# A mixture-of-experts layer on one core: three shared groups ahead of the routed slots instead of four, five row buffers, and part of the routing moved from GpSimd to VectorE

## The chip, the core and the metric

The kernel runs on one core of a Trainium2 chip. The metric is the device time of one execution in microseconds (us). Before the change the median of three runs is 888.17 us (885.1 to 893.15). PE is TensorE (its matmuls), PEld its weight loads, DVE is VectorE, ACT is ScalarE, POOL is GpSimd, SP is SyncE, which here only issues transfers.

## What is computed

`x` has 4096 tokens of 256 values (two sequences of 2048). Three steps follow each other:

```
x = x + 0.5 * ffn(layernorm(x))          # layer 0 of the code
x = x + attn(layernorm(x))               # "attention": projection, 4-tap convolution, linear recursion, silu, projection
x = x + 0.5 * ffn(layernorm(x))          # layer 1, same weights as layer 0

ffn(x):  shared = silu(x @ wg.T) * (x @ wu.T) @ wd.T          # every token
         logits = x @ gate_w.T ; e = argmax ; score = sigmoid(max)
         routed = the same form with the weights of expert e, on x * score   # 8 experts, one per token
         return shared + routed
```

## The kernel before

**Groups.** The tokens are 32 tiles of 128, in 8 groups of 4 tiles (`NG = 8`, `GT = 4`). Every product is made of three matmuls (`mm3`, lines 383 to 385: high by high, low by high, high by low part of float32 values), so PE has most of the work. The shared part of a feed-forward layer takes one group at a time: gate and up products in four blocks `fb`, then the down product, then DVE adds it to `acc` (`add_shared`). `ORDER[L]` sets the order of the groups in layer L. The first group of each order is computed while the layer norms of the others are still being made; `half_groups(L, 0)` are then computed ahead of the routed slots, and `half_groups(L, 1)` behind them.

**Routed slots.** Tokens are sorted by expert in DRAM. A place in `xs_sorted` is worked out for each token: DVE makes the one-hot table, PE the prefix sums, DVE the sums over tiles (`slot_tables`), POOL the place itself (`token_rows`, table `pos`). SP loads a group's normalized rows from `xn_kept` into one of two buffers of `rows` (`load_rows`), DVE multiplies them by the score (`scale_rows`, at the places that `SCALED` names), POOL scatters them by four indirect transfers per group (`scatter`). When the last scatter has landed, SP loads the first slots and PE starts on the 39 slots of 128 rows (`routed_slots`). The results go to `ys_sorted`.

**The weights of an expert** come twice, as raw values (`wr_raw`) and rounded ones (`wr_hi`); the low part `wr_lo` is their difference. For expert 0 POOL makes it in three parts between scatters (`cut_part`, line 1757), for the others whole (`cut_expert`, line 1765).

**Gathers.** Behind the slots POOL gathers each tile's routed rows and adds them into `acc` (line 1792), 32 tiles per layer. In layer 1 the three groups that are computed last go into a buffer of their own (`yr`, line 1901), and DVE adds them (`add_rows`). In layer 0, 24 tiles are gathered before the loop of the attention, and 8 in its first rounds (`gather(3)` whole in round 0, the tiles of group 7 in rounds 1 to 4). Each engine runs its own instructions in the order written; they wait for each other by semaphores alone.

## Time and profile before

| | |
|---|---|
| median of 3 runs | 888.17 us (885.1 to 893.15) |
| profiled execution | 891.24 us, its span 889.4 us |
| PE busy | 843.3 us, 95% of the span |
| DVE, ACT, POOL busy | 480.9, 382.1, 460.8 us |
| mean granted TensorE clock | 0.986 |

The span runs from the first to the last instruction of the core. A row of the timeline has its start, the time that it took, engine, line, output and inputs, and in brackets the idle time before it with what ended that time. A group of the lines view has the summed time and the mean of one in ns, then the idle time before the instructions. A granted clock of 1.00 is 2.4 GHz, 0.50 is 1.2 GHz.

### The profile page before, as it was taken

Reading aid. Unit: us, or ns where it says so; the run is one execution under the profiler, and the core shown is the slowest. Engines: PE = TensorE matmul, PEld = TensorE weight load, DVE = VectorE, ACT = ScalarE, POOL = GpSimd, SP = SyncE. Lnnn points to the kernel's source line nnn. Section 1 sums busy time; section 2 is a strip of 40 time slices with the busy share of each in tenths; the row PEclk is TensorE's granted clock in tenths of the full one; section 3 lists DMA queues with packets and bytes.
Section 4 is the critical chain, followed back from the end, with each engine's and each line's share of the span. In section 5 each row is a group of like instructions: output and inputs, shape, how many; then the busy total and the mean of one; then the engine's idle time right before and its main releaser. Section 6 shows DMA issues by size and latency. Waiting matters only on the chain.

```text
span 889.4 us, 16359 instructions
## 1 busy us (share of the span) xinstructions
PE 843.3 (95%) x5398; PEld 734.9 (83%) x5399; DVE 480.9 (54%) x1012; ACT 382.1 (43%) x749; POOL 460.8 (52%) x427
## 2 busy tenths in 40 slices
PE   3999989999999999998998999999999999999993
PEld 2788878888888888887887988988888888888883
DVE  6987553333333335668998885856333333333452
ACT  3353223333333333456776776333243443434230
POOL 5627670333333008869999983477331233330685
PEclk9999999999999999997999999999999999999997
DMA  9795663445555316222011016457445555521566
GB/s 309 259 327 172 204 221 109 159 163 197 189 199 191 101 50 114 40 42 30 17 45 31 24 45 223 123 189 244 167 132 189 200 189 201 177 70 35 107 150 153
DMA packets 72695, 128.66 MB, mean 145 GB/s; under 512 B 6746, under 2 KB 64228, under 8 KB 68292
## 3 DMA queue, kind: packets, MB, share of 16 engines
q0 software_dynamic: 17536, 74.33, 26.9%
q1 hardware_dynamic: 54610, 53.63, 19.1%
q8 instruction: 32, 0.52, 0.3%
q14 instruction: 19, 0.16, 0.1%
q10 hardware_dynamic: 498, 0.02, 0.0%
HBM read 91.64 MB, written 36.32 MB: 144 GB/s over the span
## 4 chain that ended last, share of the span: by engine, by line
PE 61%; POOL 15%; DVE 8%; DMA 7%; issue 5%; ACT 2%; ACTq 0%; POOLq 0%; SPq 0%; DVEq 0%
PE bank L383 18%; PE bank L384 17%; PE bank L385 17%; POOL acc L1792 5%; PE bank L591 4%; POOL xs_sorted L1725 3%; DMA rows<-xn_kept 2%; DVE v L1429 2%; DMA xs_sorted<-rows,pos 2%; DMA wr_hi<-w_routed 2%; PE bank L560 2%; POOL v L1697 2%; PE bank L450 2%; POOL wr_lo L1765 1%; POOL yr L1901 1%
## 5 line engine op out<-in xcount | busy, mean ns | idle before, releaser
L1765 POOL TENSOR_TENSOR wr_lo<-wr_raw,wr_hi 128x3072 fp32r<-128x3072 f32 x14 | 95.3, 6807 | 95.9 <-DMA wr_hi<-w_routed 92.1
L383 PE MATMUL bank<-wr_hi,xT_hi 128*128 x312 | 130.2, 417 | 1.6 <-POOL wr_lo L1765 1.5
L384 PE MATMUL bank<-wr_hi,xT_lo 128*128 x312 | 123.8, 397 | 0.0
L385 PE MATMUL bank<-wr_lo,xT_hi 128*128 x312 | 122.9, 394 | 0.0
L1134 DVE TENSOR_TENSOR hT_lo<-bank,hT_hi 128x512 fp32r<-128x512 f32 x78 | 53.9, 692 | 124.8 <-ACT hT_hi L843 124.8
L1387 DVE TENSOR_TENSOR hf<-sg,bank 128x512 f32<-128x512 f32 x78 | 53.7, 689 | 125.1 <-PE bank L385 125.1
L1792 POOL DMA_INDIRECT acc<-ys_sorted,pos x52 | 86.6, 1664 | 54.2 <-DMA ys_sorted<-rows 39.8
L383 PE MATMUL bank<-xT_hi,ws_hi 128*128 128x512 f32 x256 | 102.2, 399 | 0.4 <-DVE ws_lo L1551 0.4
L384 PE MATMUL bank<-xT_hi,ws_lo 128*128 128x512 f32 x256 | 100.6, 393 | 0.0
L385 PE MATMUL bank<-xT_lo,ws_hi 128*128 128x512 f32 x256 | 100.5, 393 | 0.0
L843 ACT ACTIVATE xT_hi<-bank 128x256 fp32r<-128x256 f32 (+1 forms) x126 | 56.0, 464 | 99.8 <-PE bank L560 88.8
L859 ACT ACTIVATE sg<-bank 128x512 f32<-128x512 f32 x64 | 38.3, 598 | 133.3 <-PE bank L385 122.3
L383 PE MATMUL bank<-wr_hi,hT_hi 128*128 x312 | 93.8, 301 | 1.3 <-DVE hT_lo L1134 1.3
L385 PE MATMUL bank<-wr_lo,hT_hi 128*128 x312 | 87.4, 280 | 0.0
L384 PE MATMUL bank<-wr_hi,hT_lo 128*128 x312 | 87.3, 280 | 0.0
L1725 POOL DMA_INDIRECT xs_sorted<-rows,pos x64 | 65.2, 1018 | 32.7 <-issue 16.8
L1429 DVE SCALAR_TENSOR_TENSOR v<-bank,vec,v 128x511 f32<-128x511 f32 (+2 forms) x96 | 71.0, 746 | 13.7 <-ACT v L992 11.1
L922 ACT ACTIVATE sg<-bank 128x512 f32<-128x512 f32 x78 | 46.6, 598 | 69.7 <-PE bank L385 69.7
L1236 DVE TENSOR_TENSOR hf<-sg,bank 128x512 f32<-128x512 f32 x64 | 43.7, 683 | 59.5 <-PE bank L385 45.5
L383 PE MATMUL bank<-ws_hi,hT_hi 128*128 128x256 f32 x256 | 74.5, 291 | 1.4 <-DVE hT_lo L1134 1.3
L384 PE MATMUL bank<-ws_hi,hT_lo 128*128 128x256 f32 x256 | 72.9, 285 | 0.0
L385 PE MATMUL bank<-ws_lo,hT_hi 128*128 128x256 f32 x256 | 72.9, 285 | 0.0
(234 smaller groups left out, 2115.1 us busy)
## 6 DMA issues: line engine op xcount, KB each, us to landing
wr_raw<-w_routed POOLq DMA_DIRECT2D x16, 1536.0 KB
wr_hi<-w_routed POOLq DMA_DIRECT2D x16, 1536.0 KB
rows<-xs_sorted SPq DMA_DIRECT2D x78, 128.0 KB, 2.6
ys_sorted<-rows SPq DMA_DIRECT2D x78, 128.0 KB, 1.7
xn_kept<-xg SPq DMA_DIRECT2D x16, 512.0 KB, 3.6
rows<-xn_kept SPq DMA_DIRECT2D x16, 512.0 KB
xg<-xn_kept SPq DMA_DIRECT2D x12, 512.0 KB
acc<-x SPq DMA_DIRECT2D x8, 512.0 KB, 9.9
```

The costliest lines, as they stand in the source:

```text
L383: pe.matmul(o, a_hi, b_hi, start=start, stop=False, skip_group_check=True)
L384: pe.matmul(o, a_lo, b_hi, start=False, stop=False, skip_group_check=True)
L385: return pe.matmul(o, a_hi, b_lo, start=False, stop=stop, skip_group_check=True)
L843: return act.activation(o, i, ACT.Copy)
L922: act.activation(sg[:, 0, :], MG[:, :], ACT.Silu).then_inc(s_msg, 1)
L1134: return dve.tensor_tensor(o, full, f32(h), ALU.subtract)
L1236: dve.tensor_tensor(hf[:, fb % 2, :], sg[:, fb % 2, :], U2[fb % 2][:, :], ALU.mult).then_inc(s_h, 1)
L1387: dve.tensor_tensor(hf[:, 0, :], sg[:, 0, :], MU[:, :], ALU.mult).then_inc(s_mh, 1)
L1429: dve.scalar_tensor_tensor(vb_[:, d:GN], UB[cb % 2][:, 0:GN - d], vec[:, cb, k:k + 1], vb_[:, d:GN], ALU.mult, ALU.add).then_inc(s_tap if ...
L1725: pool.indirect_dma_start(out=xs_dram, out_offset=bass.IndirectOffsetOnAxis(ap=pos[:, tt:tt + 1], axis=0), in_=rows[:, half * GT + t, :], ...
L1765: pool.tensor_tensor(wr_lo[:, e % 2, :], wr_raw[:, :], f32(wr_hi[:, e % 2, :]), ALU.subtract).then_inc(s_wl, 1)
L1792: pool.indirect_dma_start(out=acc[:, tt, :], out_offset=None, in_=ys_dram, in_offset=bass.IndirectOffsetOnAxis(ap=pos[:, tt:tt + 1], axis= ...
```

## The change

- `half_groups`: three groups of each layer are computed ahead of the slots and four behind (before: four and three). The orders stay.
- Five row buffers take the place of two: the two of `rows`, and three in `more_rows`, which lies where the low part of the second expert's weights comes later. SP loads the rows of groups 2 to 4 without waiting for a scatter; groups 5 to 7 wait for the scatter of the group five before.
- POOL makes only two steps of the places (`token_ranks`), and starts them from the sums over tiles. DVE makes the rest, four instructions at the end of `slot_tables`, and a new semaphore releases the scatters.
- The three parts of expert 0's low part are made by DVE in `shared_group` (`CUT`), not by POOL. The rounded weights of expert 1 are loaded after group 5's scatters, its raw ones after the last.
- DVE scales rows at other places (`SCALED`).
- In layer 0, 28 tiles are gathered before the loop of the attention, and one tile of group 3 in each of the rounds 0 to 3. In layer 1, two groups go through `yr` instead of three.

```diff
+    ROW_RING = 5
...
-        def half_groups(L, half): return ORDER[L][1:NH + 1] if half == 0 else ORDER[L][NH + 1:]
+        def half_groups(L, half): return ORDER[L][1:NH] if half == 0 else ORDER[L][NH:]
+
+        def row_buffer(g):
+            b = g % ROW_RING
+            return rows[:, b * GT:(b + 1) * GT, :] if b < 2 else more_rows[:, (b - 2) * GT:(b - 1) * GT, :]
+
+        def row_uses(L, g): return L * len(range(g % ROW_RING, NG, ROW_RING)) + g // ROW_RING
...
 
-        LATE = half_groups(1, 1)
-        ADDED = [{}, {3: (LATE[0],)}, {2: (LATE[1],), FB: (LATE[2],)}]
-
-        GATHERED = (6, 7, LATE[0], 0, LATE[1], 1, LATE[2], 2)
+        LATE = half_groups(1, 1)[2:]
+        ADDED = [{}, {}, {}, {1: (LATE[0],), FB: (LATE[1],)}]
...
-                dve.tensor_scalar(ne[:, 2, :], before, float(P), None, ALU.mult).then_inc(s_cum, 1)
+                chained(dve.tensor_scalar(ne[:, 2, :], before, float(P), None, ALU.mult))
                 dve.tensor_copy(after_e[:, :], src[0:1, :])
+                t3 = pfx[:, 0, :, :]
+                dve.wait_ge(s_rank, L + 1)
+                chained(dve.tensor_tensor(t3, t3, ne[:, 2:3, :].to_broadcast([P, NT, E]), ALU.add))
+                chained(dve.tensor_tensor(t3, t3, oh[:, :, :], ALU.mult))
+                chained(dve.tensor_reduce(m2[:, :], t3, AX.X, ALU.add))
+                dve.tensor_copy(pos[:, :], m2[:, :]).then_inc(s_pos, 1)
                 return src
...
+                        if (i, fb) in CUT:
+                            cut_part(L, CUT[i, fb])
...
+                dve.wait_ge(s_rl[g % ROW_RING], 16 * (row_uses(L, g) + 1))
                 for t in range(GT):
-                    r = rows[:, half * GT + t, :]
+                    r = row_buffer(g)[:, t, :]
                     ins = dve.tensor_scalar(r, r, score[:, bass.ds(g * GT + t, 1)], None, ALU.mult)
                 ins.then_inc(s_scl, 1)
 
...
 
-            SCALED = ([{3: (0,), FB: (1,)}, {1: (2,), 3: (3,)}, {0: (4,), 2: (5,), FB: (6,)}, {1: (7,)}],
-                      [{1: (0,), 2: (1,)}, {1: (2,), 3: (3,)}, {0: (4,), 2: (5,), FB: (6,)}, {1: (7,)}])
+            SCALED = ([{2: (0,), 3: (1,), FB: (2,)}, {0: (3,), 1: (4,), 3: (5,)}, {0: (6,), 1: (7,)}],
+                      [{1: (0,), 2: (1,), 3: (2,), FB: (3,)}, {0: (4,), 2: (5,), FB: (6,)}, {1: (7,)}])
+
+            CUT = {(1, FB): 0, (2, 0): 1, (2, 2): 2}
+
+            def cut_part(L, i):
+
+                if i == 0:
+                    dve.wait_ge(s_wraw, 16 * (L * E + 1))
+                    dve.wait_ge(s_wh, 16 * (L * E + 1))
+                ws = slice(i * W // 3, (i + 1) * W // 3)
+                ins = dve.tensor_tensor(wr_lo[:, 0, ws], wr_raw[:, ws], f32(wr_hi[:, 0, ws]), ALU.subtract)
+                if i == 2:
+                    ins.then_inc(s_wl, 1)
 
...
 
-            def token_rows(L):
+            def token_ranks(L):
 
                 pool.wait_ge(s_cum, L + 1)
                 t3 = pfx[:, 0, :, :]
                 row_step(pool.tensor_tensor(t3, t3, cum[:, 0, :, :], ALU.add))
-                row_step(pool.tensor_tensor(t3, t3, pfx[:, 1, :, :], ALU.subtract))
-                row_step(pool.tensor_tensor(t3, t3, ne[:, 2:3, :].to_broadcast([P, NT, E]), ALU.add))
-                row_step(pool.tensor_tensor(t3, t3, oh[:, :, :], ALU.mult))
-                d = E // 2
-                while d >= 1:
-                    row_step(pool.tensor_tensor(t3[:, :, 0:d], t3[:, :, 0:d], t3[:, :, d:2 * d], ALU.add))
-                    d //= 2
-                row_step(pool.tensor_copy(pos[:, :], t3[:, :, 0:1].squeeze(2)))
+                pool.tensor_tensor(t3, t3, pfx[:, 1, :, :], ALU.subtract).then_inc(s_rank, 1)
 
             def scatter(L):
...
-                    half, n = g % 2, L * NG + g
-                    pool.wait_ge(s_scl, n + 1)
+                    pool.wait_ge(s_scl, L * NG + g + 1)
                     for t in range(GT):
                         tt = g * GT + t
                         pool.indirect_dma_start(
                             out=xs_dram, out_offset=bass.IndirectOffsetOnAxis(ap=pos[:, tt:tt + 1], axis=0),
-                            in_=rows[:, half * GT + t, :], in_offset=None).then_inc(s_sct[half], 16)
-
-                    if g in (1, 3, 5):
-                        cut_part(L, g // 2)
-                    if g == 3:
+                            in_=row_buffer(g)[:, t, :], in_offset=None).then_inc(s_sct[g % ROW_RING], 16)
+                    if g == 5:
                         load_hi(L, 1)
-                    if g == 6:
-                        load_raw(L, 1)
 
             def load_raw(L, e):
...
                 load_expert(L, 0)
-                token_rows(L)
+                token_ranks(L)
                 scatter(L)
+                load_raw(L, 1)
                 if L == 0:
                     pool.wait_ge(s_wsl, 2)
-                pool.wait_ge(s_hl, 4 * (L * NG + NH + 1))
+                pool.wait_ge(s_hl, 4 * (L * NG + NH))
+                for g in range(NG - ROW_RING, NG):
+                    if g % ROW_RING >= 2:
+                        pool.wait_ge(s_sct[g % ROW_RING], 64 * (row_uses(L, g) + 1))
                 cut_expert(L, 1)
...
             gather(0, s_ga[0])
+            gather(1, s_ga[1])
+            pool.wait_ge(s_add, 2 * (c_s(0, NH) + 1))
             gather(NH, s_ga[NH])
-            gather(1, s_ga[1])
+            gather(2, s_ga[2])
+            pool.wait_ge(s_step, 16)
+            conv_bias(0)
+            pool.wait_ge(s_add, 2 * (c_s(0, NH + 1) + 1))
+            gather(NH + 1, s_ga[NH + 1])
             ln2_rsqrt(0)
             ln2_rsqrt(1)
-            pool.wait_ge(s_add, 2 * (c_s(0, NH + 1) + 1))
-            gather(NH + 1, s_ga[NH + 1])
-            pool.wait_ge(s_step, 16)
-            conv_bias(0)
-            gather(2, s_ga[2])
+            gather(NG - 1, s_ga[NG - 1])
+            pool.wait_ge(s_add, 2 * (c_s(0, NH + 2) + 1))
             ln2_rsqrt(2)
-            pool.wait_ge(s_add, 2 * (c_s(0, NH + 2) + 1))
             gather(NH + 2, s_ga[NH + 2])
             for n in range(NG + 4):
...
-                if 1 <= n <= GT:
-                    gather_tile(NG - 1, n - 1, s_ga[NG - 1])
+                if n < GT:
+                    if n == 0:
+                        pool.wait_ge(s_add, 2 * NG)
...
-                if n == 0:
-                    pool.wait_ge(s_add, 2 * NG)
-                    gather(3, s_ga[3])
...
+                for g in range(2, ROW_RING):
+                    load_rows(L, g)
...
                     sp.wait_ge(s_zero, 16 * ZERO_STORES)
-                if n >= 2:
-                    sp.wait_ge(s_sct[g % 2], 64 * (n // 2))
-                sp.dma_start(rows[:, g % 2 * GT:(g % 2 + 1) * GT, :], tiles(xn, g)).then_inc(s_rl[g % 2], 16)
+                if L == 0 and g == 2:
+                    sp.wait_ge(s_wsl, 2)
+                if L == 1 and g == 2:
+                    sp.wait_ge(s_vb, 4 * NG)
+                if g >= ROW_RING:
+                    sp.wait_ge(s_sct[g % ROW_RING], 64 * row_uses(L, g))
+                sp.dma_start(row_buffer(g), tiles(xn, g)).then_inc(s_rl[g % ROW_RING], 16)
 
             def shared_load(L, i):
```

POOL in layer 0, from the loads of expert 0 to the low part of expert 1, before (`xs_sorted<-rows,pos` is a scatter, `pos` the table of places):

```order
L1743 DMA wr_hi<-w_routed 128x3072
...
L1714 TENSOR_TENSOR pfx<-pfx 128x32
L1716 CAST pos<-pfx 128x32
L1725 DMA xs_sorted<-rows,pos 4992x256 x8
L1757 TENSOR_TENSOR wr_lo<-wr_raw,wr_hi 128x1024
L1725 DMA xs_sorted<-rows,pos 4992x256 x8
L1757 TENSOR_TENSOR wr_lo<-wr_raw,wr_hi 128x1024
L1743 DMA wr_hi<-w_routed 128x3072
L1725 DMA xs_sorted<-rows,pos 4992x256 x8
L1757 TENSOR_TENSOR wr_lo<-wr_raw,wr_hi 128x1024
L1725 DMA xs_sorted<-rows,pos 4992x256 x4
L1740 DMA wr_raw<-w_routed 128x3072
L1725 DMA xs_sorted<-rows,pos 4992x256 x4
```

The same place of the changed kernel:

```order
L1746 TENSOR_TENSOR pfx<-pfx,cum 128x256
L1747 TENSOR_TENSOR pfx<-pfx 128x256
L1756 DMA xs_sorted<-rows,pos 4992x256 x8
L1756 DMA xs_sorted<-more_rows,pos 4992x256 x12
L1756 DMA xs_sorted<-rows,pos 4992x256 x4
L1769 DMA wr_hi<-w_routed 128x3072
L1756 DMA xs_sorted<-rows,pos 4992x256 x4
L1756 DMA xs_sorted<-more_rows,pos 4992x256 x4
L1766 DMA wr_raw<-w_routed 128x3072
```

The number of scatters is the same, 32. What stood between them is down to one load.

DVE in the first group ahead of layer 0's slots, before, from the end of the tables to the first scaled rows (line 1236 is a product of the gate, 1134 the low part of its result, 1246 to 1251 copies of the setup):

```order
L1222 CAST after_e<-ne 1x8
L1236 TENSOR_TENSOR hf<-sg,bank 128x512
...
L1230 CAST slot_e<-sef 1x39
L1134 TENSOR_TENSOR hT_lo<-hf,hT_hi 128x512
L1236 TENSOR_TENSOR hf<-sg,bank 128x512
L1246 COPY kpad<-bank 1x256
...
L1251 TENSOR_TENSOR kpad<-kpad,dd 1x1
L1134 TENSOR_TENSOR hT_lo<-hf,hT_hi 128x512
L1357 TENSOR_SCALAR rows<-rows,score 128x256 x4
```

The same place of the changed kernel:

```order
L1239 CAST after_e<-ne 1x8
L1242 TENSOR_TENSOR pfx<-pfx,ne 128x256
L1243 TENSOR_TENSOR pfx<-pfx,oh 128x256
L1244 TENSOR_REDUCE m<-pfx 128x32
L1245 CAST pos<-m 128x32
L1259 TENSOR_TENSOR hf<-sg,bank 128x512
...
L1253 CAST slot_e<-sef 1x39
L1147 TENSOR_TENSOR hT_lo<-hf,hT_hi 128x512
L1383 TENSOR_SCALAR rows<-rows,score 128x256 x4
L1259 TENSOR_TENSOR hf<-sg,bank 128x512
```

Four instructions are new, and the first scaling has moved ahead of a product, the copies of the setup and a low part.

POOL at the end of layer 1, before (`acc<-ys_sorted,pos` gathers and adds, `yr<-ys_sorted,pos` only gathers):

```order
L1792 DMA acc<-ys_sorted,pos 128x256 x8
L1901 DMA yr<-ys_sorted,pos 128x256 x4
L1792 DMA acc<-ys_sorted,pos 128x256 x4
L1901 DMA yr<-ys_sorted,pos 128x256 x4
L1792 DMA acc<-ys_sorted,pos 128x256 x4
L1901 DMA yr<-ys_sorted,pos 128x256 x4
L1792 DMA acc<-ys_sorted,pos 128x256 x4
```

And in the changed kernel:

```order
L1769 DMA wr_hi<-w_routed 128x3072
L1781 TENSOR_TENSOR wr_lo<-wr_raw,wr_hi 128x3072
L1812 DMA acc<-ys_sorted,pos 128x256 x20
L1922 DMA yr<-ys_sorted,pos 128x256 x4
L1812 DMA acc<-ys_sorted,pos 128x256 x4
L1922 DMA yr<-ys_sorted,pos 128x256 x4
```

There are 32 tiles in both; the last of them now belong to a group that DVE adds.

## Rows read from the trace of the kernel before

**Rows 1.** Windows: us, busy (count) by engine, PEclk, DMA share, GB/s.

```profile
405.00:414.50 9.50, 9.28 (x37) 8.43 (x38) 8.61 (x10) 3.85 (x10) 8.99 (x11) 0.51 0.12 16
414.50:485.00 70.50, 66.61 (x476) 58.83 (x476) 60.05 (x127) 51.27 (x110) 66.92 (x92) 1.00 0.12 30
...
560.00:628.00 68.00, 68.00 (x400) 60.26 (x399) 44.06 (x99) 21.47 (x38) 46.03 (x46) 1.00 0.57 186
```

**Rows 2.** Timeline of PE: waits, the groups' transposes, the last matmul.

```profile
131.23 0.69 PE L560 MATMUL bank<-ident,rows 128*128 128x128 f32 x2 [3.35 <-DMA rows<-xs_sorted]
...
402.55 0.49 PE L383 MATMUL bank<-xT_hi,win_hi 128*128 128x512 f32 x1 [2.77 <-DVE xT_lo L1134]
...
588.81 1.04 PE L450 MATMUL bank<-ident,xg 128*128 128x128 f32 x8
...
606.35 1.03 PE L450 MATMUL bank<-ident,xg 128*128 128x128 f32 x8
...
629.04 0.44 PE L560 MATMUL bank<-ident,rows 128*128 128x128 f32 x2 [0.69 <-DMA rows<-xs_sorted]
...
875.70 0.28 PE L385 MATMUL bank<-ws_lo,hT_hi 128*128 128x256 f32 x1
```

**Rows 3.** Timeline of POOL, first and last scatter of layer 0.

```profile
68.84 1.28 POOL L1725 DMA_INDIRECT xs_sorted<-rows,pos  x1 [1.32 <-DVE rows L1357]
...
125.48 1.29 POOL L1725 DMA_INDIRECT xs_sorted<-rows,pos  x1 [0.30 <-issue]
```

**Rows 4.** POOL by lines, 68 to 127 us, layer 0.

```profile
L1725 POOL DMA_INDIRECT xs_sorted<-rows,pos x32 | 33.3, 1040 | 17.6 <-DVE rows L1357 9.3 <-issue 8.3
L1757 POOL TENSOR_TENSOR wr_lo<-wr_raw,wr_hi 128x1024 fp32r<-128x1024 f32 x3 | 7.2, 2397 | 0.1
L1743 POOL DMA_DIRECT2D wr_hi<-w_routed x1 | 0.6, 608 | 0.0
```

**Rows 5.** POOL by lines, 569 to 624 us, layer 1.

```profile
L1725 POOL DMA_INDIRECT xs_sorted<-rows,pos x32 | 31.9, 996 | 15.1 <-issue 8.5 <-DVE rows L1357 5.5 <-POOL pos L1716 1.0
```

**Rows 6.** Timeline of POOL, last scatter of layer 1.

```profile
622.90 0.96 POOL L1725 DMA_INDIRECT xs_sorted<-rows,pos  x1 [0.30 <-issue]
```

**Rows 7.** Timeline of DVE, layer 0, the tables and the first scaling.

```profile
60.03 0.42 DVE L1212 TENSOR_REDUCE ne<-cmp_t 128x8 f32<-128x256 f32 x1
...
64.07 0.69 DVE L1236 TENSOR_TENSOR hf<-sg,bank 128x512 f32<-128x512 f32 x1
...
66.66 1.28 DVE L1357 TENSOR_SCALAR rows<-rows,score 128x256 f32<-128x256 f32 x4
```

**Rows 8.** Timeline of DVE, layer 1, behind the tables.

```profile
563.68 1.27 DVE L1284 SCALAR_TENSOR_TENSOR acc<-bank,acc 128x512 f32<-128x512 f32 x2
...
565.48 2.50 DVE L1357 TENSOR_SCALAR rows<-rows,score 128x256 f32<-128x256 f32 x4
```

**Rows 9.** Timelines of POOL and DVE: subtractions of two tiles in SBUF beside POOL.

```profile
18.72 3.17 POOL L1633 TENSOR_TENSOR rstd<-ve,mhalf 128x4 f32<-128x4 f32 x1
18.75 2.24 DVE L1551 TENSOR_TENSOR ws_lo<-ws_raw,ws_hi 128x2048 fp32r<-128x2048 f32 x1
...
106.63 0.96 POOL L1725 DMA_INDIRECT xs_sorted<-rows,pos  x1 [4.60 <-DVE rows L1357]
106.86 0.69 DVE L1134 TENSOR_TENSOR hT_lo<-hf,hT_hi 128x512 fp32r<-128x512 f32 x1
```

**Rows 10.** POOL by lines, 394.4 to 522 us, and its first idle row after them.

```profile
L1792 POOL DMA_INDIRECT acc<-ys_sorted,pos x8 | 13.6, 1703 | 1.7 <-issue 1.6
...
522.14 1.29 POOL L1701 TENSOR_TENSOR hT_lo<-v,hT_hi 128x512 fp32r<-128x512 f32 x1 [1.34 <-ACT hT_hi L843]
```

**Rows 11.** Timelines of DVE and SP at the end.

```profile
877.20 1.29 DVE L1284 SCALAR_TENSOR_TENSOR acc<-bank,acc 128x512 f32<-128x512 f32 x2
...
877.92 0.97 SPq L2022 DMA_DIRECT2D out<-acc  x2
883.30 0.37 SPq L2025 DMA_DIRECT2D out<-acc  x1
```

More of the change, by code:

```diff
@@ L295, in build @@
         s_ga = [sem(f"gathered{g}") for g in range(NG)]
-        s_fin = [sem(f"last_gathered{g}") for g in range(NG)]
         s_fad = sem("gathered_rows_added")
@@ L1973, in first_loads @@
                     sp.dma_start(HV[:, :], bass.AP(k_dram, 0, [[1, P], [1, CH]])).then_inc(s_hank, 16)
-                for g in range(2, NG):
+                for g in range(ROW_RING, NG):
                     load_rows(L, g)
-                    if L == 0 and g == 3:
+                    if L == 0 and g == ROW_RING:
                         sp.wait_ge(s_flv, 1)
@@ L2003, in _ @@
             routed_slots(0)
+            shared_load(0, 4)
             shared_load(0, 5)
```

69 lines of the change are left out of this document (35 added, 34 removed).

## The prediction, made before the changed kernel was run

> **What bounds the kernel now.** I read the windows by stage first. TensorE is busy in nearly all of them: from 560 to 628 us, the four groups ahead of layer 1's slots, it is busy 68.00 of 68.00 us at full clock [rows 1]. So a change that moves no matmul away can only win or lose in the few places where PE waits. The timeline of PE with its waits shows them. The first transposes of the slots waited 3.35 us in layer 0 and 0.69 us in layer 1 for sorted rows, and the attention waited 2.77 us at 402.55 [rows 2]. In 414.5 to 485 PE was idle 70.50 - 66.61 = 3.9 us [rows 1]. The last place is the end: the last matmul starts at 875.70 [rows 2], but the last store is issued at 883.30 [rows 11] and the span ends at 889.4. There POOL's gathers are behind, not PE.
>
> One group costs PE a fixed time, from transposes to transposes 606.35 - 588.81 = 17.54 us [rows 2]. The change takes 17.54 us from the front of the slots and puts it behind them. This is worth something at the end, where POOL gets 17.54 us more cover, and it costs something at the front, where the scatters lose the same cover. The question is whether the scatters are now done 17.54 us earlier.
>
> **Front, layer 0.** Before, the first scatter started at 68.84 and the last at 125.48, 56.6 us for 32 [rows 3]. In between lay 7.2 us of low parts, 9.3 us of waiting for scaled rows and a load of 0.6 us [rows 4]. An undisturbed scatter takes 0.96 us and 0.30 us pass before it, 1.27 us together as started [rows 6]. No buffer and no other engine makes that shorter, and the 32 scatters stay. The new chain is:
> - 31 x 1.27 = 39.4 us from the first start to the last;
> - the mean was 1.04 us, not 0.96 [rows 4]: 32 x 0.08 = 2.6 us;
> - the load of expert 1's rounded weights, 0.6 + 0.3 = 0.9 us [rows 4];
> - three low parts on DVE. Two tiles in SBUF are subtracted; 2048 columns took 2.24 us, so 1024 take about 1.1 us. The rows beside POOL differ. A small POOL step that met such a subtraction took 3.17 us [rows 9]; but a scatter that began 0.23 us ahead of another took its plain 0.96 us [rows 9]. The price of one is between 0 and 1.2 us; I take 0.6, three are 1.8 us.
>
> That is 44.7 us. The start: the first scaling began at 66.66. It is moved ahead of what DVE did from 64.07, which is 2.6 us earlier [rows 7], and behind four new instructions. Three of them work on 256 columns, like the reduction of 0.42 us [rows 7], with a semaphore step between, so 3 x 0.46 + 0.2 = 1.6 us; I add 0.3 us for POOL's two steps. The scaling begins at 66.0 and ends at 67.3. Before, the scatter started 68.84 - (66.66 + 1.28) = 0.9 us after it [rows 3, 7]; I take 0.6, so 67.9. The last scatter starts at 67.9 + 44.7 = 112.6, and the transposes came 131.23 - 125.48 = 5.75 us after it [rows 2, 3]: 118.35. Before they came at 131.23, less one group 113.69. **Layer 0 loses 4.7 us.** Row loads don't bind this chain: groups 2 to 4 are loaded without waiting, and group 5 needs only the scatters of group 0, some 25 us ahead. The delays of PE's products by DVE's new work fall in the same stretch and are hidden by the chain; without it they would cost up to some 2 us. The low part of expert 1, now made after the last scatter, is hidden by expert 0's slots.
>
> **Front, layer 1.** The same: 39.4 + 32 x 0.036 = 1.2 [rows 5] + 0.9 + 1.8 = 43.3 us. The scaling began at 565.48 and took 2.50 us [rows 8] with POOL's steps beside it. Now it begins 1.6 us later, at 567.1, takes 1.28 us as in layer 0 [rows 7], and the first scatter starts at 569.0. The last starts at 612.3, and 629.04 - 622.90 = 6.14 us later [rows 2, 6], at 618.4, the transposes. Before, less one group: 611.5. **Layer 1 loses 6.9 us.** Here the lost waits were smaller, 5.5 us [rows 5], so less is taken out of the chain. POOL needs about 43 us for its scatters however they are fed, and three groups are too short a cover for that.
>
> **Clock.** PE will stand still some 8 us in front of each layer's slots. The trace has one stretch of such a kind: after the 2.77 us of waiting at 402.55 the granted clock was 0.51 for 9.5 us [rows 1, 2], 1.2 GHz; that costs up to 4.75 us. After the 0.69 us in layer 1 nothing of it shows. The start of the slots is full of short waits, which hide a part. Between 0 and 4.75 us for each layer I take 1.2: **loss 2.4 us.**
>
> **Attention.** Eight gathers stood among POOL's work there, 1.70 us each and up to 0.30 between [rows 10]; four remain, one of them ahead of the first rows that POOL waits for. POOL was never idle up to 522.14 [rows 10], so its lateness is what PE's 3.9 us of idle time in 414.5 to 485 answer to. The 2.77 us come from DVE and stay, and the clock behind them too. Bounds: nothing, if DVE is late next (60.05 of 70.50 us busy [rows 1]), and 5 x 1.85 = 9.2 us. I take the idle time and a little before it: **gain 4.5 us.** The other gathers, 28 tiles at 1.85 us or 52 us ahead of the loop, lie beside four groups, 70 us.
>
> **End.** The gathers of layer 1 take 24 x 1.85 + 8 x 1.27 = 54.6 us, and begin some 5 us after PE's last slot; they end ahead of PE's 70 us. So the chain is: last matmul until 876.0, DVE's half of the last addition 0.65 us [rows 11], store issued at about 877.0. From 883.30 the last store took 6.1 us to the end of the span; it has half the bytes now, 5.5 us. The end comes at 882.5, **a gain of 6.9 us** (4 if one more gather is late by 3 us, 7.5 if the half store takes 4.9).
>
> **Sum.** 4.7 + 6.9 + 2.4 - 4.5 - 6.9 = +2.6 us. The profiled execution took 891.24 us, which becomes 893.8; it was 3.1 us above the median, so the median goes from 888.17 to 890.8 us. A difference under 1%, 8.9 us, is no change that this measurement can tell with certainty.
>
> **Rivals.**
> 1. *A clock that stays low at the slots (slower).* PE's wait in front of each layer's slots is about 8 us, longer than the one at 402.55. If each is followed by 9.5 us at 0.51, the two cost 9.5 us and not 2.4: +9.7 us, 897.9 us. For it: the attention's stretch. Against it: after 3.35 us of waiting in layer 0 no such long stretch followed. It decides the sign beyond 1% from about 4.3 us per layer. Chance 0.15.
> 2. *The low parts block the scatters wholly.* Every one meets a scatter's start and costs its length and a bit, 1.2 us: 6 x 0.6 = 3.6 us more, 894.4 us. For: the step of 3.17 us [rows 9]. Against: the scatter that began first [rows 9]. The Trainium skill has this as a rule (SBUF — State Buffer, "SBUF: two separate sides"): a DVE operation with two SBUF inputs and a GpSimd operation that reads SBUF take a shared port pair as an exclusive lock, whichever starts first, and the other is blocked fully. By that rule the 0.6 us of the sum would be 1.2. The row of 3.17 us agrees; the pair at 106.63 is in line with it only if the DVE instruction needed no lock, since its 0.69 us were not lengthened. Chance 0.12.
> 3. *The waits stay (the change doesn't do what it says).* Rows of groups 2 to 4 come late behind other transfers, or DVE scales them late, and POOL waits as before, 9.3 and 5.5 us [rows 4, 5]: +17.4 us, 905.6 us. Against: three of these loads no longer wait for a scatter. Chance 0.05.
> 4. *POOL was the attention's bound throughout, and nothing is lost beside the chain (faster).* The gain there is 9.2 us, the low parts and the clock cost nothing: 2.6 - 4.7 - 3.6 - 2.4 = -8.1 us, 880.1 us. Chance 0.16, and about two in three of that lies below 879.3.
>
> My forecast has 0.52. The range takes in the clock's rival and the fast one down to 881: **881 to 899 us**. Faster by over 1% 0.13, within 1% 0.68, slower by over 1% 0.19.
>
> **What would show it.** In the changed kernel's trace 32 scatters should run in about 45 and 43 us, with next to no wait for rows; the first transposes of the slots near 118 and 618 us minus what layer 0 shifted, each behind a wait of about 8 us; POOL idle sooner than before in the attention; the last store about 1 us behind the last matmul. The forecast is wrong if scatters come closer than 1.27 us, if those waits are under 4 us, or if PE's idle time in the attention is still 3.9 us.

## The result: slower by 2.55%, 911.88 us

| | median (runs) | ratio to before, 95% interval |
|---|---|---|
| before | 886.64 us (885.1 to 893.15, 4) | |
| changed | 911.88 us (910.44 to 913.88, 4) | 1.0255 (1.0219 to 1.029) |

The forecast was 890.8 us, with a range of 881 to 899, so it missed by 21 us. Between the profiled executions the miss is 17 us (911.06 against 893.8); the rest is that the one of before was 3.1 us above its median and this one 0.8 us below. The profiled execution of the changed kernel took 911.06 us, its span 908.9 us (before 891.24 and 889.4), at a mean granted clock of 0.977 (0.986).

To see where the time is, I cut both spans at events of TensorE: the prefix sums of the routing (56.00 and 57.30 us), the first and last transposes of the slots, the first and last products of the attention, the last matmul. In the rows "less a group" the front of the kernel before is counted without the group that the change moves away, 17.54 us [rows 2]. The last column is a later trace of the same changed kernel, told of below.

| us, changed less before | forecast | result's trace | second trace |
|---|---|---|---|
| start-up up to the routing | 0 | +1.3 | +1.3 |
| front of layer 0 less a group | +4.7 | **+14.1** | +5.9 |
| attention | -4.5 | -7.1 | -6.0 |
| front of layer 1 less a group | +6.9 | **+19.9** | +10.3 |
| both layers' slots (clock) | +2.4 | +1.5 | +0.9 |
| behind the last matmul | -6.9 | -10.2 | -10.2 |
| sum | +2.6 | +19.5 | +2.3 |

The miss is in the two fronts. The other four rows together are -14.5 us, against a forecast of -9.0. The start-up differs between executions of one kernel (0.2 us less than before in another trace of the changed one).

### The profile page after: what moved, and what is told of

It reads as the page before. It is cut to its first block, busy times and chain, and to the rows that moved or that the text cites. A ratio compares the mean times of both kernels' runs of the same rounds, so it can differ in the third digit from the quotient of the medians.

```text
span 908.9 us, 16358 instructions
## 1 busy us (share of the span) xinstructions
PE 853.4 (94%) x5398; PEld 741.9 (82%) x5399; DVE 484.2 (53%) x1025; ACT 382.7 (42%) x749; POOL 446.9 (49%) x409
## 4 chain that ended last, share of the span: by engine, by line
PE 76%; DVE 10%; DMA 5%; another core or an unknown queue 4%; POOL 2%; issue 2%; ACT 1%; ACTq 0%; SPq 0%; DVEq 0%; POOLq 0%
PE bank L396 22%; PE bank L398 22%; PE bank L397 22%; PE bank L604 4%; DVE v L1467 3%; PE bank L463 2%; PE bank L573 2%; DVE stats L1158 2%; DMA rows<-xn_kept 2%; POOL xs_sorted L1756 1%; DMA rows<-xs_sorted 1%; DMA wr_hi<-w_routed 1%; POOL wr_lo L1781 1%; DMA xs_sorted<-more_rows,pos 1%
## 5 line engine op out<-in xcount | busy, mean ns | idle before, releaser
L1812 POOL DMA_INDIRECT acc<-ys_sorted,pos x56 | 91.5, 1634 | 63.8 <-DMA ys_sorted<-rows 39.7
L396 PE MATMUL bank<-xT_hi,ws_hi 128*128 128x512 f32 x256 | 104.6, 409 | 8.9 <-DVE hf L1259 8.5
L872 ACT ACTIVATE sg<-bank 128x512 f32<-128x512 f32 x64 | 38.3, 598 | 161.8 <-PE bank L398 118.9
L1259 DVE TENSOR_TENSOR hf<-sg,bank 128x512 f32<-128x512 f32 x64 | 43.8, 684 | 96.9 <-PE bank L398 54.8
L396 PE MATMUL bank<-ws_hi,hT_hi 128*128 128x256 f32 x256 | 76.8, 300 | 2.7 <-issue 2.1
L398 PE MATMUL bank<-ws_lo,hT_hi 128*128 128x256 f32 x256 | 74.9, 293 | 2.9 <-issue 2.7
L397 PE MATMUL bank<-ws_hi,hT_lo 128*128 128x256 f32 x256 | 75.0, 293 | 1.4 <-issue 1.4
L1147 DVE TENSOR_TENSOR xT_lo<-bank,xT_hi 128x256 fp32r<-128x256 f32 (+1 forms) x126 | 63.3, 518 | 17.2 <-ACT xT_hi L856 17.1
```

Of the source, the lines that this page charges most:

```text
L396: pe.matmul(o, a_hi, b_hi, start=start, stop=False, skip_group_check=True)
L397: pe.matmul(o, a_lo, b_hi, start=False, stop=False, skip_group_check=True)
L398: return pe.matmul(o, a_hi, b_lo, start=False, stop=stop, skip_group_check=True)
L872: act.activation(sg[:, fb % 2, :], G2[fb % 2][:, :], ACT.Silu).then_inc(s_sg, 1)
L1147: return dve.tensor_tensor(o, full, f32(h), ALU.subtract)
L1259: dve.tensor_tensor(hf[:, fb % 2, :], sg[:, fb % 2, :], U2[fb % 2][:, :], ALU.mult).then_inc(s_h, 1)
```

## The profile after

The first places answer to [rows 2] and [rows 11]: TensorE's timeline with its waits, the first transposes of the slots in both layers, the attention's wait, and the last matmul; then SP's last stores, which join the half store to the one before.

```profile
129.07 0.69 PE L573 MATMUL bank<-ident,rows 128*128 128x128 f32 x2 [4.22 <-DMA rows<-xs_sorted]
...
418.14 0.80 PE L396 MATMUL bank<-xT_hi,win_hi 128*128 128x512 f32 x1 [2.77 <-DVE xT_lo L1147]
...
639.89 0.62 PE L573 MATMUL bank<-ident,rows 128*128 128x128 f32 x2 [3.23 <-DMA rows<-xs_sorted]
...
905.34 0.28 PE L398 MATMUL bank<-ws_lo,hT_hi 128*128 128x256 f32 x1
```

```profile
904.29 2.46 SPq L2049 DMA_DIRECT2D out<-acc  x2
```

The slots' transposes came at 129.07 and not at 118.35, though TensorE waited only 4.22 us for the rows, not 8: it was late itself. Windows over the two fronts, the kernel before first, then the changed one, show both parts of that, idle time and a lower granted clock (us, busy by engine, clock, DMA):

```profile
90.00:112.00 22.00, 20.68 (x130) 18.53 (x129) 11.75 (x24) 5.67 (x10) 14.01 (x14) 1.00 0.63 203
590.00:625.00 35.00, 35.00 (x209) 31.16 (x208) 19.69 (x41) 11.04 (x21) 24.64 (x24) 1.00 0.73 246
```

```profile
90.00:112.00 22.00, 16.67 (x82) 14.48 (x83) 12.56 (x27) 5.35 (x12) 10.90 (x11) 0.77 0.45 145
590.00:625.00 35.00, 24.52 (x110) 20.64 (x109) 12.89 (x24) 5.66 (x10) 20.54 (x21) 0.80 0.49 166
```

The end went as forecast, and further: the span ends 3.6 us behind the last matmul's start.

GpSimd's lines from 69 to 122 us and from 569 to 632 us answer to [rows 4, 5]. There are 16 scatters from `rows` and 16 from `more_rows` in each.

```profile
L1756 POOL DMA_INDIRECT xs_sorted<-rows,pos x16 | 18.6, 1162 | 19.7 <-DVE rows L1383 15.7 <-issue 4.0
L1756 POOL DMA_INDIRECT xs_sorted<-more_rows,pos x16 | 15.5, 971 | 4.9 <-issue 4.9
...
L1756 POOL DMA_INDIRECT xs_sorted<-rows,pos x16 | 18.4, 1147 | 19.6 <-issue 10.7 <-DVE rows L1383 9.0
L1756 POOL DMA_INDIRECT xs_sorted<-more_rows,pos x16 | 16.2, 1014 | 5.5 <-issue 4.6 <-DVE more_rows L1383 0.9
```

The waits for scaled rows have not gone. Those of layer 0 hold the wait ahead of the first scatter too, 6.8 us; the rest is 7.38 and 1.58 us. In layer 0 the chain starts at 69.45, runs through 20 scatters without a gap, and stops:

```profile
93.14 0.97 POOL L1756 DMA_INDIRECT xs_sorted<-more_rows,pos  x1 [0.30 <-issue]
94.42 0.97 POOL L1756 DMA_INDIRECT xs_sorted<-more_rows,pos  x1 [0.30 <-issue]
102.77 0.96 POOL L1756 DMA_INDIRECT xs_sorted<-rows,pos  x1 [7.38 <-DVE rows L1383]
```

VectorE scaled these rows late, since it waited itself. Its timeline, ScalarE's (L872 is the silu of a gate product) and TensorE's in the same stretch:

```profile
90.49 0.69 DVE L1259 TENSOR_TENSOR hf<-sg,bank 128x512 f32<-128x512 f32 x1 [5.96 <-issue]
...
98.98 0.69 DVE L1259 TENSOR_TENSOR hf<-sg,bank 128x512 f32<-128x512 f32 x1 [7.21 <-ACT sg L872]
...
101.36 1.14 DVE L1383 TENSOR_SCALAR rows<-rows,score 128x256 f32<-128x256 f32 x4
```

```profile
85.94 0.62 ACT L856 ACTIVATE hT_hi<-hf 128x512 fp32r<-128x512 f32 x1
98.30 0.60 ACT L872 ACTIVATE sg<-bank 128x512 f32<-128x512 f32 x1 [11.73 <-remote]
```

```profile
85.90 0.39 PE L398 MATMUL bank<-xT_lo,ws_hi 128*128 128x512 f32 x1
...
91.23 0.80 PE L396 MATMUL bank<-xT_hi,ws_hi 128*128 128x512 f32 x1 [3.58 <-DVE hf L1259]
...
100.82 0.45 PE L463 MATMUL bank<-ident,xg 128*128 128x128 f32 x1 [4.10 <-ACT qq L856]
```

This is the strange place. The last matmul of the gate product starts at 85.90 and takes 0.39 us. ScalarE, which has nothing else to do from 86.56 on, begins its silu at 98.30: 12.4 us later. "Remote" is what the trace writes where it finds no releaser near the wait's end. I call the time from the start of the matmul that carries an increment to the start of the instruction that waits for it, where that instruction's engine was free, the **lag**. It is 0.43 us in the median for gate and up products. The trace models the ends of matmuls, so it can't tell a late increment from a late end of the matmul that carries it; I call both a late increment. In this trace six gate lags and six up lags are over 1 us, all in or just behind long runs of scatters. The largest is 12.4 us in layer 0, in a run of 20, and 18.2 us in layer 1, in a run of 24. These two end when the run has ended, 3.9 us after its last scatter has started (94.42 to 98.30) and 4.5 us (608.85 to 613.37). Others come through late while the run goes on (593.58 and 597.89). In the trace of before the largest are 2.2 us (at 92.1) and 1.9 us (at 579.1), each behind a run of 8 scatters.

So the chain of causes in the result's trace is: late increment of TensorE, late silu, late product, VectorE (in order) late with the rows of group 5, GpSimd idle, and TensorE waiting for `hf` and `qq` meanwhile, at a lower granted clock.

## Experiments

The theories: **A**, a long unbroken run of scatters holds back TensorE's increments; **B**, VectorE's added work makes it late; **C**, three groups are too short a cover and no more; **D**, the lateness belongs to the chip or the execution, not to the changed order. D came up when the second kernel ran. The kernels ran in six sessions on six different chips, one session to a chip, so each ratio is to the kernel before of its own session; "chip" below stands for both, as no chip was seen twice. Kernels of different sessions are compared by their times alone.

### Pauses in the run of scatters

```diff
+                    if g in (1, 3, 5):
+                        pause(4)
```

`pause(4)` is four memsets of a scratch tile, one after the other.

> The changed kernel with one addition: GpSimd pauses after the scatters of groups 1, 3 and 5 (four memsets of a scratch tile, by the rows of the changed kernel some 0.45 us each, with semaphore steps about 2.3 us together). So its unbroken runs of scatters have 8 and not 20 or 24. Theory A (an unbroken run of scatters holds back TensorE's semaphore increments): no increment arrives more than about 2.5 us late (now up to 12.4 in layer 0, 18.2 in layer 1), PE's waits of 3.6 and 4.1 us (layer 0) and 3.5 us (layer 1) go, POOL's waits of 7.4 and 9.0 us for scaled rows go, and though 7 us of pauses are added to each chain of scatters the time falls or stays: 903 to 911 us. Theory B (the added work on VectorE makes it late with scaling): the lateness stays, the pauses are hidden in part by the waits for rows: 912 to 920 us. Theory C (three groups are too short a cover and nothing else): the chains grow by 7 us each less the waits of 9 us that they replace, 912 to 926 us.

Measured: 904.45 us, ratio 1.016 (1.0126 to 1.0194), no lag over 1 us. This looked like theory A's cure. It was none: as the later runs showed, the changed kernel takes 893 us on a chip of this kind, and the pauses cost what they add. The session had no run of the changed kernel itself in it, and that was my error.

### The front part of the change alone

```diff
-        def half_groups(L, half): return ORDER[L][1:NH] if half == 0 else ORDER[L][NH:]
+        def half_groups(L, half): return ORDER[L][1:NH + 1] if half == 0 else ORDER[L][NH + 1:]
```

> The front part of the change alone: five row buffers, early scaling, the places and the low parts on VectorE, but four groups ahead of the slots and three behind as before, and the gathers as before. Here the scatters have more cover than they need, so what TensorE loses it loses by other things. Theory A: the scatters again run 20 or more in one go, the gate and up increments of PE come up to 12 to 18 us late, PE waits for hf, qq or banks some 4 to 8 us in each layer and runs slower behind that; the time is 895 to 903 us, slower than before, although the waits of 3.35 and 0.69 us ahead of the slots are gone. Theory B: VectorE's added work costs about 2 us in each layer, the waits ahead of the slots go: 885 to 889 us. Theory C: 883 us, 4 us faster than before.

Measured: 887.55 us, ratio 0.9975 (0.9945 to 1.0004). All 32 scatters ran with no wait, the last at 111.89 us, and no lag was over 1 us. A as stated (every chip, any run over 8) falls. The time lies in B's band, and TensorE's timeline shows B's true size: it waited for VectorE 1.65 us at 69.22, for the copies of the setup that now stand behind a scaling, and for `hf` 0.56 us at 64.53 and 0.86 us at 564.51: some 3 us, nothing like the 21 us of the miss. With four groups the front part is worth 0 to 0.5%: TensorE's own work lasts until 128 us anyway.

### The split alone

```diff
-        def half_groups(L, half): return ORDER[L][1:NH + 1] if half == 0 else ORDER[L][NH + 1:]
+        def half_groups(L, half): return ORDER[L][1:NH] if half == 0 else ORDER[L][NH:]
```

This edit is against the kernel before: two row buffers, the places and the low parts on GpSimd stay, the gathers and the end are those of the changed kernel.

> The other part alone: three groups ahead of the slots and four behind, with the gathers and the end as changed, but two row buffers, the places and the low parts on GpSimd and scatters as before (56.6 and about 52.6 us for 32, in runs of at most 8). Worked out from the rows: both fronts lose the whole group of 17.5 us of cover (+17.5, +16.9), the attention gives 7.4 and the end 8.9: 887 + 18.1 = 905 us. Theory A says 903 to 909 us with no increment of PE later than about 2.5 us, so the front's part of the change made the kernel slower and not faster beside it. Theories B and C say that the front's part was worth something, so that this kernel is slower than the changed one: above 912 us, 918 if the scatters alone were 6 us shorter.

Measured: 908.44 us, ratio 1.0188 (1.015 to 1.0226). The sum from rows, 905, held within 3.5 us. Theory A's second half, that the front part made the kernel slower beside this, fell with the next session: the changed kernel has a ratio of 1.0014 there, so the front part is worth some 15 us where three groups are all the cover (908.44 against 893.68 us, on two chips).

### The low parts back on GpSimd

```diff
-            CUT = {(1, FB): 0, (2, 0): 1, (2, 2): 2}
+            CUT = {}
...
+                    if g in (1, 3, 5):
+                        cut_part(L, g // 2)          # on GpSimd
```

> The changed kernel with one part undone: the three parts of expert 0's low part are made by GpSimd again, after the scatters of groups 1, 3 and 5 (2.4 us each), and not by VectorE. They break the run of scatters as the pauses do, and take work from VectorE. Theory A: like the kernel with pauses, within 2 us of it, 903 to 911 us. Theory B: VectorE's three subtractions were the cause; this kernel gains and the one with pauses does not, 903 to 909 us here against 912 or more there. Theory C: chains longer by 7.2 us each less the waits that they replace, 912 to 926 us.

Measured: 904.55 us, 1.0162 (1.0128 to 1.0196), within 0.1 us of the kernel with pauses. Against 893.7 us for the changed kernel on such chips, moving the three low parts gained 5 us or so in each layer, less than the 7.2 us that they take on GpSimd.

### The changed kernel again

> The changed kernel word for word, once more, beside the kernel before. The run of the front part alone had 32 scatters with hardly a gap and no late increment, which speaks against theory A as it stood. Theory A1 (the late increments belong to the changed kernel's own order): the trace shows them again, 4 to 18 us late in both layers, with POOL's waits of 7 and 9 us; 909 to 914 us. Theory D (they belong to the chip or the execution of that one trace, and the change itself costs less): no increment later than about 2 us, the first scatter near 68 and not 69.5, the last scatter near 112 in layer 0, no waits for scaled rows over 2 us; 893 to 904 us.

> The kernel before word for word, once more, for a trace from the same chip as the changed kernel's second one. Theory D: the small late increments of its first trace (1.9 us at 579.1, 2.24 us at 92.1) are gone or elsewhere; span within 2 us of 889.4. Theory A1: they are at the same places, behind the same runs of eight scatters.

Measured: the changed kernel **893.68 us** (892.24 to 894.13), ratio 1.0014 (0.9996 to 1.0032); the kernel before in one run 885.78 us. No lag in either trace is over 0.7 us. The same instructions as at 85.90 and 98.30 above, from TensorE and ScalarE:

```profile
86.02 0.39 PE L398 MATMUL bank<-xT_lo,ws_hi 128*128 128x512 f32 x1
```

```profile
86.44 0.60 ACT L872 ACTIVATE sg<-bank 128x512 f32<-128x512 f32 x1 [3.85 <-PE bank L398]
```

12.4 us have become 0.42, with the same 20 scatters in a row (69.56 to 94.67). The same program in the same places, so the lateness isn't in the program alone. (The first scatter came at 69.56 all the same and not near 68, and the run goes on to 24.) GpSimd's line now has no wait behind the first scatter (the 6.8 us are those ahead of it), and the slots' transposes wait for rows as forecast:

```profile
L1756 POOL DMA_INDIRECT xs_sorted<-rows,pos x16 | 17.3, 1082 | 11.4 <-DVE rows L1383 6.8 <-issue 4.6
```

```profile
120.97 0.69 PE L573 MATMUL bank<-ident,rows 128*128 128x128 f32 x2 [8.14 <-DMA rows<-xs_sorted]
...
622.37 0.69 PE L573 MATMUL bank<-ident,rows 128*128 128x128 f32 x2 [10.16 <-DMA rows<-xs_sorted]
```

### More gathers through the buffer at the end

```diff
+        VIA = (6, 7) + LATE                          # gathered into yr, added by VectorE
```

> The front part alone (four groups ahead of the slots), and at the end five groups instead of three gathered into a buffer of their own and added by VectorE: groups 6 and 7 too. A plain gather started every 1.27 us and one that adds every 1.85 us, so GpSimd's 32 gathers end 8 x 0.58 = 4.6 us sooner; VectorE gets two additions of 1.2 us, beside TensorE's work. If the gathers are what the end waits for (before: last matmul 875.7, last store 883.3), the time falls by 3.5 to 4.6 us against the front part alone: 883 to 884 us. If the last store or VectorE's additions bound the end, nothing: 887 us.

Measured: **885.11 us**, ratio 0.9918 (0.9892 to 0.9943). The last gather started 2.9 us sooner than in the front part alone, not 4.6: some plain gathers took 1.3 to 1.9 us beside the stores.

### Two more chips, a single pause, two buffers

> The changed kernel word for word, a third time, in a call of its own and so perhaps on another chip. On the chip of its second run it took 893.68 us and TensorE's increments were never late; in its first trace, 911 us, they were up to 18 us late in both layers. Theory D1 (the lateness belongs to some chips, not to the program): here it is either about 893 us with no increment over 2 us late, or about 911 us with late ones behind the long runs of scatters, all executions of a chip alike. Theory D2 (it comes and goes from execution to execution): times of both kinds in one call. Theory D3 (it belonged to the first loading alone): 892 to 896 us.

> The changed kernel with one pause of some 2.3 us on GpSimd, after the scatters of group 3, so that they go in runs of 16 and 16. Where increments are not late, the scatter chain ends 2.3 us later in each layer and the time is 4 to 5 us above the changed kernel's on the same chip (898 us). Where they are late (theory D1, a chip that shows it), the first run of 16 still holds some back for up to 5 us, the pause lets them through, and the time is below the changed kernel's (903 to 908 against 911).

> The front part alone once more (four groups ahead of the slots), 887.55 us on its first chip with all 32 scatters in one run and no late increment. Theory D1: on a chip where the changed kernel shows late increments this one shows them too, with waits of TensorE for hf, qq or banks, 895 to 903 us; on a chip where it shows none, 885 to 889 us.

Measured: 893.92 us, ratio 1.0053 (1.0031 to 1.0075); one pause 897.78 and the front part alone 886.74, one run each. No lag over 1 us in any. A pause of 2.3 us in each layer costs 4 us.

```diff
-    ROW_RING = 5
+    ROW_RING = 2
```

> The changed kernel word for word, a fourth time, in a new call. It took 893.68 and 893.92 us on two chips with no late increment of TensorE, 911.88 us in its first runs with increments up to 18 us late. Theory D1 (the lateness belongs to a chip): here all executions are near 893 or all near 911. Theory D2 (it comes and goes between executions): both in one call. Theory D3 (to the first loading alone): 891 to 897 us.

> The changed kernel with one part undone: two row buffers instead of five, everything else kept (places and low parts on VectorE, three groups ahead). A group's rows are then loaded only when the scatters of the group two before have landed. From the rows of the kernel before, a scatter lands some 3 us after its start, a load and the scaling take about 3 and 1.3 us, so a pair of groups takes 12.6 us instead of 10.2: GpSimd waits about 2.5 us for each of the three later pairs, 7 to 8 us in each layer, and the time is about 14 us above the changed kernel's, 905 to 912 us. If the buffers had only replaced waits that others would have caused anyway (theory B, VectorE late), 893 to 898 us.

Measured: changed 892.65 us, ratio 1.0009 (0.9971 to 1.0047), on a fourth chip without lateness; two buffers 910.81 us (two runs). The buffers are worth 18 us with three groups ahead, somewhat more than the 14 expected: the waits for scaled rows are 13.7 us in layer 0 and 7.2 us in layer 1.

### The lateness again, and twice the scatters

```diff
+                        pool.indirect_dma_start(     # behind each scatter: 128 rows of zeros, same places
+                            out=x2_dram, ..., in_=ident2[:, :], ...).then_inc(s_dup, 16)
```

> The changed kernel word for word, a fifth time, in a new call: 893.68, 893.92 and 892.65 us so far on three chips without a late increment, 911.88 us in its first runs with late ones. Theory D1 (some chips show the lateness): all executions near 893 or all near 911. Theory D3 (the first loading alone): 891 to 897 us.

> The front part alone (four groups ahead of the slots), with a second scatter behind each of the 32: 128 rows of zeros into a spare table by the same places, so 64 scatters in one run, twice the suspected load. The output stays complete, the spare table is not used. The chain gets 32 x 1.27 = 41 us longer in each layer, about 10 us of it are covered: 887 + 62 = 949 us, of no interest. What counts are the increments. Theory A2 (a long run of scatters holds back TensorE's increments on every chip, from a length that 32 does not reach here): some come over 2 us late in the later half of the run. Theory D (it is a matter of the chip or the loading): all stay at 0.43 us, and none over 1 us.

> The front part alone with five groups gathered through the buffer, once more on another chip: 885.11 us on the first, 0.9918 of the kernel before. All theories: 884 to 887 us, 0.5 to 1.1% under the kernel before, unless this chip shows late increments (D1), then 893 us or more.

Measured: the fifth chip shows it. The changed kernel took **910.07 us** (two runs), ratio 1.0228 (1.0175 to 1.0281), with lags up to 12.2 and 18.2 us at the same places as in the result's trace. The kernel before was at 890.66 us there, no slower than elsewhere. The form with four groups, 885.11 us before, took **916.72 us**, ratio 1.0294 (1.0235 to 1.0353), with lags up to 18.1 us. With doubled scatters one run took 993.74 us, 45 us more than expected. Its first unbroken run of layer 0 has 40 scatters, and the lag grows with it. The last matmul of a gate product starts at 84.35, and ScalarE sees it 5.7 us after the last scatter of that run has started; GpSimd and ScalarE there:

```profile
118.33 0.97 POOL L1762 DMA_INDIRECT xs_spare<-spare_rows,pos  x1 [0.30 <-issue]
128.66 0.97 POOL L1759 DMA_INDIRECT xs_sorted<-rows,pos  x1 [9.36 <-DVE rows L1386]
```

```profile
124.02 0.60 ACT L875 ACTIVATE sg<-bank 128x512 f32<-128x512 f32 x1 [36.81 <-remote]
```

A lag of 39.7 us, and 43.8 us in layer 1, where the run has 48. So theories A and D are both half right: on some chips TensorE's increments are held back while scatters follow each other. Doubling them doubles GpSimd's instructions and their transfers alike; which of the two holds the increments back, no run separates.

### A cure, on a chip that needs it

> The changed kernel with GpSimd's pauses of 2.3 us after the scatters of groups 1, 3 and 5, once more: 904.45 us on a chip without late increments, where the pauses only lengthen the chains (893 us plus 5 in each layer). Theory D1 with A (on chips like that of the first runs, a run of 20 and more scatters holds back TensorE's increments, runs of 8 hardly): on such a chip this kernel stays at 903 to 908 us and is faster than the changed kernel there (910), with no increment over 2.5 us late. If the pauses don't cure it, 915 us or more. On a chip without lateness 903 to 906 us.

> The changed kernel word for word, to tell which kind of chip this call has: about 893 us with all increments in time, or about 911 us with late ones up to 18 us in both layers.

The last kernel takes the four-group form with the buffer, makes the low parts on GpSimd between the scatters, and puts adding gathers between the plain ones:

```diff
-        GATHERED = (6, 7, LATE[0], 0, LATE[1], 1, LATE[2], 2)
+        GATHERED = (6, 0, 7, LATE[0], 1, LATE[1], LATE[2], 2)
```

> A version made from the findings: four groups ahead of the slots, five row buffers and the places on VectorE as changed, but the low parts made by GpSimd between the scatters (so that these go in runs of 8), and five groups gathered through the buffer with an adding gather between them (6, 0, 7, ...), so that the plain gathers go in runs of at most 8. The chain is 7 us longer than with the low parts on VectorE, 117 instead of 112 us in layer 0, and the four groups cover it (PE needs them until 128). Without late increments: 884 to 887 us. Theory D1 with A: the same on a chip that shows lateness, 884 to 890 us, where the unpaced form took 916.72. If the runs' length is not the cause there: 905 us or more.

Measured, on the sixth chip, which shows lateness too: changed 910.04 us (one run), lags up to 17.8 us; with pauses 906.52 us (two runs), lags up to 3.0 us; the paced form **885.39 us**, ratio 0.9943 (0.9916 to 0.997), lags up to 3.0 us. The pauses gain 3.5 us here, with one and two runs behind the difference, though they cost 11 us elsewhere. What they show clearly is the lag, 3.0 us instead of 17.8 on the same chip, a little over the 2.5 expected. The paced form is 31 us faster than the unpaced one on the other such chip and equal to it where there is no lateness; the two never ran on one chip. GpSimd's lines of its layer 0 up to 121 us show no wait but the one ahead of the first scatter:

```profile
L1747 POOL DMA_INDIRECT xs_sorted<-rows,pos x16 | 16.8, 1049 | 11.6 <-DVE rows L1384 7.0 <-issue 4.6
...
L1776 POOL TENSOR_TENSOR wr_lo<-wr_raw,wr_hi 128x1024 fp32r<-128x1024 f32 x3 | 7.2, 2403 | 0.1
```

All of it together:

| chips | changed | four groups | the same with `VIA` | with `VIA`, paced | changed with pauses | largest lag of the changed |
|---|---|---|---|---|---|---|
| four | 893.68, 893.92, 892.65 | 887.55, 886.74 | 885.11 | not run | 904.45 | under 1 us |
| two | 910.07, 910.04 | not run | 916.72 | 885.39 | 906.52 | 18.2 us |

The result's own runs, 911.88 us, belong to the second row by time and by lags.

## Why the prediction was wrong, step by step

**The step that failed** is the one that set TensorE's and VectorE's delays aside: "the delays of PE's products by DVE's new work fall in the same stretch and are hidden by the chain", and with it that no other wait enters the chain. I asked who else works beside the scatters, not what the scatters do to others. A run of 20 to 24 without a gap was new; before, none had more than 8. On chips like that of the result it cost 8.2 us in front of layer 0 and 9.6 in front of layer 1, against the second trace. That is nearly the whole difference between 911 and 894. Two more traces with late increments have +12.7 and +13.8 us in front of layer 0 and +19.6 and +20.5 in front of layer 1, two more without them +5.8 and +5.9, and +10.5 in both. The trace of before held a hint, two lags of about 2 us behind runs of 8, which no group of lines shows; they are seen only by matching each wait with the matmul that it waits for.

**Rival 3** (the waits stay, 905.6 us, 0.05) named the right symptom: 9.0 and 9.9 us of waits for scaled rows instead of 9.3 and 5.5 [rows 4, 5]. Its causes, late row loads or too much work on VectorE, were wrong, and its chance was too low.

**The chain's length** was right: from first to last scatter 43.1 and 44.2 us in the second trace, forecast 44.7 and 43.3. A scatter and a low part on VectorE met at 94.67:

```profile
94.67 2.03 POOL L1756 DMA_INDIRECT xs_sorted<-more_rows,pos  x1 [0.30 <-issue]
```

```profile
94.63 1.22 DVE L1409 TENSOR_TENSOR wr_lo<-wr_raw,wr_hi 128x1024 fp32r<-128x1024 f32 x1
```

The scatter takes 0.97 us alone. Here it took as long as the rest of the subtraction (until 95.85) and 0.85 us more. Where the other two fell, the next scatters took 1.33 and 1.59 us. Together that is 1.06 + 0.36 + 0.62 = 2.0 us in layer 0, forecast 1.8; rival 2 (3.6 us more) fell on its price, since a part meets a scatter at any point of its length. Its mechanism held one way round. The Trainium skill (SBUF — State Buffer, "SBUF: two separate sides") says that whichever of the two starts first has the shared ports for its whole instruction. Where the subtraction starts first these rows agree: each late scatter ends 0.84 or 0.85 us behind it. Where the scatter starts first they don't. In layer 1 a low part that began 0.33 us behind one took its plain 1.22 us:

```profile
597.32 0.96 POOL L1756 DMA_INDIRECT xs_sorted<-more_rows,pos  x1 [0.30 <-issue]
```

```profile
597.65 1.22 DVE L1409 TENSOR_TENSOR wr_lo<-wr_raw,wr_hi 128x1024 fp32r<-128x1024 f32 x1
```

In the prediction's row of 3.17 us, too, the GpSimd step started 0.03 us ahead and was still the one that waited [rows 9].

**From the last scatter to the transposes** I took 5.75 and 6.14 us; it was 8.3 and 8.1 us. SP issued the slots' loads at 115.20, 2.5 us after the last scatter, but they needed 5.8 us instead of 2.0. The raw weights of expert 1, 1536 KB and 7.0 us to landing, had been issued at 113.67, ahead of them. The change had moved this load behind the last scatter; the sum had nothing for its transfer. That is read from the traces; no run moved the load alone.

**The clock.** I took 1.2 us for each layer. After waits of 8.1 and 10.2 us the granted clock was 0.50 for the first 3.7 and 4.0 us of the slots, which costs 1.8 and 2.0 us; the slots as a whole were only 0.9 us longer than in the trace of before, where the clock had fallen at the slots of layer 0 too. Rival 1, 9.5 us at half clock for each, fell.

**Attention** -6.0 to -7.1, forecast -4.5. The mechanism was right, GpSimd's lateness; its size was not. In the stretch that answers to 414.5 to 485 of [rows 1], TensorE was idle 0.9 us in the result's trace (2.0 us in the second) and no longer 3.9:

```profile
418.10:430.00 11.90, 11.86 (x70) 10.70 (x71) 11.35 (x21) 8.88 (x20) 11.40 (x12) 0.86 0.08 12
430.00:500.00 70.00, 69.10 (x502) 61.71 (x501) 65.72 (x128) 53.62 (x114) 66.25 (x97) 1.00 0.10 28
```

I had held the low clock behind the 2.77 us wait for a cost that stays. The second trace of the kernel before has a shorter one (0.86 over 12 us, where the first has 0.57) and needs the same 149.76 us for the attention, with 5.8 us idle instead of 3.9. So the clock cost nothing there, as far as two traces show; GpSimd set the pace. That is rival 4's mechanism; its 9.2 us were not reached.

**The end** -10.2, forecast -6.9: the last half store is issued about 1 us behind the last matmul as forecast, but the span ends 2.5 us later and not 5.5.

On the three chips without lateness where the changed kernel ran, it took 892.65 to 893.92 us, ratios 1.0009 to 1.0053: the forecast of 890.8 us was right within 3.1 us, and so was "within 1%". That the total came so close is in part luck. Against the second trace the fronts' losses were too small by 1.2 and 3.4 us and the start-up's 1.3 us were missing; the gains of the attention and the end were too small by 1.5 and 3.3 us, and the clock's loss too large by 1.5, which nearly cancels. The range did not hold the result because nothing in it stood for late increments, which differ from chip to chip.

## What to carry to other kernels

When an edit removes the small works between GpSimd's indirect transfers, look at who waits for TensorE in that stretch, and match waits with matmuls: on some chips its increments came up to 18.2 us late in runs of 20 to 24, and 3.0 us at most in runs of 8. Leave work of GpSimd between them when the chain is covered anyway; it costs nothing and keeps the time alike on all chips. And put the changed kernel itself into every session of experiments: without it a pause that cost 11 us looked like a cure that gained 7.

## What the hardware showed that I had not expected

- On two of six chips, and in the result's runs, an increment of TensorE reached ScalarE and VectorE up to 18.2 us late during 20 to 24 scatters in a row, 43.8 us late with the scatters doubled. On the other four no lag was over 1 us, and the median was the same 0.43 us. What sets those chips, or their sessions, apart stays open.
- An increment of VectorE came in time in the same stretch: its product of 90.49 to 91.18 let TensorE start at 91.23.
- Scatters in runs of 8 with 2.4 us of other work between them kept the lag to 3.0 us or less. GpSimd's adding gathers, one every 1.85 us, showed none over 1 us in runs of 20 (changed kernel, layer 1); behind 12 plain gathers, one every 1.25 us, and the mixed ones after them, lags up to 5.6 us appeared on the fifth chip.
- The kernel before took 890.66 and 890.54 us on the two chips, 889.67 to 892.31 us on the others: a kernel can be blind to it.
